# Loads of the probability exchange: quarters of the source rows to all 128 partitions, instead of 32 partitions from all rows

## What is computed

```python
def attention(q, w_qkv, w_dense):
    qkv = q @ w_qkv.T                    # 4096 query, 1024 key, 1024 value columns
    ...
    scores = jnp.einsum('bskgd,btkd->bkgst', qh, kh) * scale
    scores = jnp.where(causal, scores, jnp.finfo(scores.dtype).min)
    probs = jax.nn.softmax(scores, axis=-1)
    attn = jnp.einsum('bkgst,btkd->bskgd', probs, vh)
    return attn.reshape(Bq, Sq, NHEADS * HEAD_D) @ w_dense.T

x = x + layernorm(attention(layernorm(x), w_qkv, w_dense))
x = x + layernorm(ffn(layernorm(x)))
```

## Time and profile before

| | |
|---|---|
| median of 3 runs | 1196.01 us (1194.56 to 1196.65) |
| the profiled execution | 1197.52 us, of which the span from first to last instruction is 1195.7 us |
| TensorE matmul busy | 1117.8 us (93%) |
| VectorE, ScalarE, GpSimd busy | 862.6, 640.3, 804.1 us |
| moved by DMA | 216.89 MB, mean 181 GB/s |
| granted TensorE clock | 0.983 of full speed |

### The profile page before, as it was taken

One profiled execution on the slowest core, in us unless ns is written; L12 is line 12 of the kernel. 1 busy time (PEld: TensorE's weight loads), 2 busy tenths in 40 slices (PEclk: granted clock), 3 DMA queues, 4 the chain that ended last, 5 costly groups with the idle time before them and its releaser, 6 DMA issues.

```text
span 1195.7 us, 16875 instructions
## 1 busy us (share of the span) xinstructions
PE 1117.8 (93%) x5218; PEld 928.2 (78%) x5218; DVE 862.6 (72%) x1698; ACT 640.3 (54%) x1237; POOL 804.1 (67%) x836
## 2 busy tenths in 40 slices
PE   8999999999989989989988989988899889999997
PEld 7888888888777767777767777867688768888885
DVE  4544546467788878788888878988667896666666
ACT  6432333258577665766766766755468642222224
POOL 7744457437859769677869579857585676656645
PEclk9999999999999999999999989989999999999999
DMA  6444664447899698797797795895430124333422
GB/s 216 137 179 145 190 211 141 143 139 221 255 270 266 200 286 250 219 301 212 257 280 235 242 286 171 265 304 150 128 98 1 53 56 146 94 116 114 119 66 94
DMA packets 157875, 216.89 MB, mean 181 GB/s; under 512 B 41056, under 2 KB 122592, under 8 KB 152928
## 3 DMA queue, kind: packets, MB, share of 16 engines
q1 hardware_dynamic: 157792, 215.89, 59.8%
HBM read 125.00 MB, written 90.83 MB: 181 GB/s over the span
## 4 chain that ended last, share of the span: by engine, by line
PE 54%; DMA 17%; DVE 13%; issue 5%; POOL 4%; ACT 3%; SPq 3%; DVEq 0%; POOLq 0%; ACTq 0%
PE psS L1586 16%; PE psOY L1586 14%; PE psT L1586 11%; DMA squares_long<-p_scr_long 10%; PE psOY L1719 7%; DMA p_scr_long<-probs_long 6%; PE psOY L1734 5%; DVE pT_lo L1242 4%; SPq L497 2%; DVE squares_long L1329 2%; PE psT L1700 2%; POOL pT_lo L662 1%; DVE probs_long L1310 1%; POOL probs_long L722 1%; DVE y L1387 1%
## 5 line engine op out<-in xcount | busy, mean ns | idle before, releaser
L1586 PE MATMUL psS<-kT_hi,qT_hi 128*128 128x384 f32 (+6 forms) x384 | 140.5, 366 | 40.6 <-DVE negmax L1310 40.3
L1329 DVE STREAM_TRANSPOSE squares_long<-squares_long 128x1792 f32<-128x1792 f32 (+3 forms) x54 | 102.2, 1893 | 62.9 <-DMA squares_long<-p_scr_long 62.9
L1036 ACT ACTIVATE probs_long<-probs_long,negmax 128x896 f32<-128x896 f32 (+9 forms) x124 | 122.4, 989 | 35.9 <-DVE negmax L1310 35.3
L722 POOL TENSOR_SCALAR probs_long<-probs_long,rsum 128x768 f32<-128x768 f32 (+9 forms) x98 | 93.2, 961 | 67.5 <-DVE rsum L1317 67.4
L662 POOL TENSOR_TENSOR pT_lo<-squares_long,pT_hi 128x896 fp32r<-128x896 f32 (+3 forms) x47 | 108.7, 2322 | 42.6 <-ACT pT_hi L1031 42.4
L1586 PE MATMUL psS<-kT_hi,qT_lo 128*128 128x384 f32 (+6 forms) x384 | 134.2, 349 | 0.0
L1586 PE MATMUL psS<-kT_lo,qT_hi 128*128 128x384 f32 (+6 forms) x384 | 134.0, 349 | 0.0
L1586 PEld LDWEIGHTS psS<-kT_hi,qT_hi 128*128 128x128 f32 x384 | 75.6, 197 | 58.1 <-issue 34.0
L1734 PE MATMUL psOY<-wd_hi,oT_hi 128*128 128x512 f32 x256 | 104.9, 410 | 10.1 <-DVE oT_lo L1242 8.7
L1031 ACT CAST pT_hi<-squares_long 128x1792 fp32r<-128x1792 f32 (+3 forms) x54 | 84.9, 1572 | 47.9 <-DVE squares_long L1329 47.6
L1242 DVE TENSOR_TENSOR pT_lo<-squares_long,pT_hi 128x896 fp32r<-128x896 f32 (+4 forms) x47 | 105.3, 2257 | 0.2 <-ACT pT_hi L1031 0.2
(11 more groups left out here) (208 smaller groups left out, 3282.6 us busy)
## 6 DMA issues: line engine op xcount, KB each, us to landing
q_raw<-q_scr SPq DMA_DIRECT2D x64, 256.0 KB, 5.3
p_scr_long<-probs_long SPq DMA_DIRECT2D x14, 896.0 KB, 6.3
squares_long<-p_scr_long SPq DMA_DIRECT2D x56, 224.0 KB, 5.7
p_scr_long<-probs_long SPq DMA_DIRECT2D x12, 1024.0 KB, 5.9
squares_long<-p_scr_long SPq DMA_DIRECT2D x48, 256.0 KB, 7.3
p_scr_long<-probs_long SPq DMA_DIRECT2D x14, 768.0 KB, 4.5
squares_long<-p_scr_long SPq DMA_DIRECT2D x56, 192.0 KB, 4.3
raw<-in_w_qk SPq DMA_DIRECT2D x10, 1024.0 KB, 6.4
```

The source lines that it names most:

```text
L722: nc.gpsimd.tensor_scalar(row, row, rsum[:, column(t, u)], 1.0, ALU.mult, ALU.mult).then_inc(p_ready[lane(t)], 1)
L1036: nc.scalar.activation(row, row, ACT.Exp, bias=negmax[:, column(t, u)], scale=-1.0, accum_out=lsum[:, column(t, u)]).then_inc(e_done[lane( ...
L1329: nc.vector.transpose(rows, rows).then_inc(swap_turned[c], 1)
L1586: last = nc.tensor.matmul(dst, a, b, start=(start and k == 0), stop=(stop and k == len(terms) - 1), skip_group_check=resumed)
```

## The change

Each of the four loads of a pack used to take one piece of `w` columns (`b`) of all 128 source rows, and wrote it to the 32 partitions of quarter `b`, in four pieces (`a`) for each partition. Now each takes a quarter (`a`) of the source rows, 32 rows, with all four pieces of each row, and writes one piece to each of the 128 partitions: partition 32 * b + q, columns a * w to (a + 1) * w, from row 32 * a + q, piece b. The same elements go to the same places. The number of loads, the length of a piece and the semaphore counts are as before. The similar loads of the feed-forward part (L610) stay as they are.

```diff
--- before.py
+++ after.py
@@ -493,10 +493,10 @@
                     sp.wait_ge(swap_lo[c], low_count(earlier, DVE_LOW, end))
                     if low_count(earlier, POOL_LOW, end):
                         sp.wait_ge(swap_lo_pool[c], low_count(earlier, POOL_LOW, end))
-                for b in range(HG):
-                    sp.dma_start(rows[b * SPAN:(b + 1) * SPAN, :].rearrange("q (a x) -> q a x", a=HG),
-                                 p_scr[c][pack_count(t, k) % 2, k, :, b * w:(b + 1) * w].rearrange("(a q) x -> q a x", a=HG)
-                                 ).then_inc(swap_in[c][k], 16)
+                for a in range(HG):
+                    sp.dma_start(rows[:, a * w:(a + 1) * w],
+                                 p_scr[c][pack_count(t, k) % 2, k, a * SPAN:(a + 1) * SPAN, 0:HG * w].rearrange(
+                                     "q (b x) -> b q x", b=HG)).then_inc(swap_in[c][k], 16)
 
             def store(kind, n, tile, done):
                 if kind == "k":
```

## The result

The changed kernel takes 1530.09 us (median of 4 runs, 1529.98 to 1530.38) against 1196.33 us (4 runs): a ratio of 1.279, 95% interval 1.2768 to 1.2813. It is slower by 334 us. The forecast was 1740 us with a range of 1480 to 2000.

A forecast was written before the change was run, and what follows sets the result against it. TensorE was taken as the bound, transfers a close second. In the exchange stage, loads 770, other transfers 247 and drains 107 us made 1124 for 580 us, +544 on 1197.5, less 1.5 for the median: 1740 us, range 1480 to 2000.

The forecast's parts named there:

- the nearest row: Profile row of the old loads, on 16 engines; it spoke for 16 engines after the change, given 0.13.
- the last rival: Exchange stage: four engines run clean at 21.3 GB/s, drains covered; 856 us for 580, 1473 us; under 1480 had 0.03.
- The signs: Expected in the changed profile: landings 12 to 25 us, DMA share near 40%, 216.9 MB, loads alone 75 GB/s, lower clock.
- The rate: Changed loads in the exchange stage: 18.4 GB/s for a busy engine, 770 us on each of four engines.
- the earlier trace: Packets of 2 KB to 128 partitions from 5 to 8 us, kernel before: 21.3 GB/s for a busy engine.
- the rival of four engines that crowd each other: Exchange stage: loads at 12.5 GB/s, 1487 us for 580, 2103 us in all; over 2000 had 0.04.
- The other transfers: Exchange stage: the other 84.0 MB still go over 16 engines at 21.3 GB/s, 247 us.
- The drains: SyncE's queue: four engines idle after each of 41 waits for a store to land, 2.6 us each, 107 us.
- The price of issuing: SyncE's queue: issuing one load was to stay at 432 ns in the middle, costing nothing more.
- The clock: TensorE in the exchange stage: at half the clock its work would be up to 1044 us, under 1124; priced at 0.
- The sixteen-engine rival: Exchange loads dealt over 16 engines at 21.3 GB/s, half of VectorE's saved wait gained, 13 us: 1183 us; chance 0.08.
- about 8 engines: Exchange stage: a gain needs more than this; with 8, loads 332 us and others make 579 us, the stage as it is.

The follow-up runs named there:

- e1_sixteen: Changed kernel, but each load reads columns of all 128 source rows, so 16 engines carry it; exchange left out: 1166.31 us, 0.9763 of the kernel before.
- e2_eight: Changed kernel, but the source is read with 8 as its outermost axis, so 8 engines; exchange left out: 1288.45 us, 1.0758 of the kernel before.
- e9_four: Changed kernel, but each of four engines reads every fourth source row; exchange left out: 1557.75 us, 1.3022 of the kernel before.
- e8_single: Changed kernel's four engines, but one load per pack instead of four; exchange left out: 1616.13 us, 1.3533 of the kernel before.
- e3_short_only: Kernel before, with the change for the short tiles' 96 loads alone: 1257.23 us, 1.0517 of the kernel before.
- e4_long_only: Kernel before, with the change for the long tiles' 216 loads alone: 1475.11 us, 1.2338 of the kernel before.
- e7_store: Kernel before, with the exchange moved to four stores of 32 partitions per pack and a single load of 128: 1188.08 us, 0.9937.

## Why the prediction was right, and where its size was off

**Direction and mechanism: right.** The step that decided was the choice between 16 engines (the nearest row) and 4 (the source's outermost axis). The changed kernel's packets show 4, and e1_sixteen, e2_eight and e9_four, in one form, put the time in the order of the engines. Among the recorded cases the nearest is not the forecast, 210 us too high, but the last rival, four engines that run clean, at 1473 us, 57 us too low.

**The signs.** The mean share of the stage (43.8% for near 40%), the bytes (216.88 MB), TensorE's slices and the lower clock came as said. Loads alone flow at 101 GB/s, not 75. The landing of 12 to 25 us can't be checked, as the profile gives no landing for these loads. And DMA is 29% of the chain, not most of it; with SyncE's queue, which stands in L497, it is 50%.

**The rate: the term that was off.** The prediction took 18.4 GB/s for a busy engine, the middle of 15.6 and 21.3; it was 24.0. So the loads take 14.16 MB / 24.0 GB/s = 590 us on each of the four, not 770. Both neighbours in the trace were poor guides. 12.5 and 15.6 GB/s are of 16 engines that crowd on 32 partitions; and the 21.3 of the earlier trace rows is not what an engine can do on 128 partitions. With 4 engines it moves 24.0, with 8 it moves 23.9 (199 / (16 x 0.52)), and with 16 also 23.8, in the first 2 us of the stretch of e1_sixteen. The trace of the kernel before had a row that says so, 2 us behind the earlier trace rows, loads to 128 partitions with pieces of 2 and 8 KB, from 10 to 12 us:

```profile
DMA packets 148, 0.83 MB, mean 417 GB/s; under 512 B 11, under 2 KB 11, under 8 KB 58
...
q1 hardware_dynamic: 148, 0.83, 99.6%
```

That is 417 / (16 x 0.996) = 26.2 GB/s. The upper end of the range of rates should have come from such a row. The rival of four engines that crowd each other (2103 us) is refuted by the 24.0 GB/s as well.

**The other transfers: right.** 247 us foreseen. The stage's share is 43.8% of 16 engines over 910 us:

```profile
q1 hardware_dynamic: 62845, 140.51, 43.8%
```

6377 engine-us, less 56.6 MB / 24.0 GB/s = 2359 for the loads, leaves 4018, or 251 us each.

**The drains: too dear.** 590 + 251 = 841 us of 910, so the four engines were idle for 69 us, for 107 foreseen. In the packets, none is in flight for 69 us of the stage, and for 72 us of the stage before: this idle time was there already and didn't grow. SyncE's waits for a store to land in L497 fell from 41 to 26 (20 + 6), though their sum rose from 93 to 155 us. The wait in L495, which I had expected to shrink, grew from 83.0 to 129.2 us; it lies beside the same transfers and isn't an addition to them.

So 770 to 590 is -180, 247 to 251 is +4, 107 to 69 is -38, together -214 us, and 1124 less 214 is the 910 us measured. The sum closes by construction, as the idle time is what is left, and it takes the rate of a stretch with loads alone for all loads; so how the difference splits between rate and idle time is an estimate.

**The price of issuing: wrongly put as unchanged.** It rose from 432 to 530 ns and, for the short tiles, to 964, and SyncE's queue from 3% to 21% of the chain. By e8_single this isn't a loss that comes on top: with a quarter of the issues the time didn't fall.

**The clock: foreseen.** TensorE's granted clock was 0.81 in the stage, and its 595 us of busy time fit into 910. Whether some of the 73 us more are on the path isn't shown, as no run holds the clock.

**The sixteen-engine rival: too small.** e1_sixteen gives 30 us, not 13. The prediction halved VectorE's waits as if those alone were the price, and missed what the experiments with a part of the work show: the loads' time on an engine is paid for the most part at any size. In one form, with 23.8, 23.9 and 24.0 GB/s, the load work on a busy engine is 149, 296 and 590 us for 16, 8 and 4 engines, and the times are 1166, 1288 and 1558 us: 122 us for 147, and 269 us for 294. (With 20.5 GB/s, the mean over the 4 us, it is 173 us for 16 engines, and the first step 122 us for 123.) The engine's idle time in the stage (for 16 engines 0.74 x 549 = 406 busy of 549, so 143 us; 69 in the changed kernel) shrinks, but gives back only a part. There is no flat part below the point at which the work on the busiest engines equals the stage's 580 us, on which I had built the expectations of e2_eight and e3_short_only, and the "about 8 engines" of the prediction: 8 engines cost 92 us.

A reason that fits is the single in-order queue: SyncE waits for a store to land, then issues its loads, and everything issued later waits behind them, so the loads of a pack are one link of a chain that closes through `probs` and `squares`. The additive losses of e3_short_only and e4_long_only, and e8_single, in which the wait moved from SyncE to the DMA queue and didn't go away, speak for it; a kernel with a second queue or more buffers, which would test it, wasn't tried.

## What to carry to other kernels

Look at the outermost axis of both sides of each DMA: a source of 4 blocks left 12 of 16 DMA engines idle here, although the other side had all 128 partitions, and the profile shows it as a low DMA share in a chain full of DMA, and as fewer small packets. Where an exchange has to touch 32 partitions at a time, issue the quarters in the order 0, 2, 1, 3, which costs nothing and gave 13 us here, and try the exchange on the store as well (19 us with that order). And don't take the time of a stage with one in-order DMA queue as the larger of its sums: price longer transfers at most of their length (here 0.8 to 0.9 of it).

## What the runs showed of the hardware

- A load dealt over 4 or 8 engines was dearer to issue than one over 16: 432 ns in the middle with 16 engines, 530 with 4. With 8 it is 575:

```profile
L497 SPq DMA_DIRECT2D squares_long<-p_scr_long x216: 574/575/1411, 281.3 to 932.4; - x108
```

- A busy engine moves about 24 GB/s of 1.8 KB pieces to 128 partitions, whether 4, 8 or 16 work (24.0, 23.9, 23.8). With 16 it didn't last: over the 4 us of the stretch the mean was 20.5. It moves 12.5 when 16 work on loads that write 32 partitions, and 15.6 when they work on stores that read 32 (e7_store).
